# Two PSUM banks for the own-row products, and the one-hots' column numbers in SBUF, in a three-layer graph network

## The reference

```python
# layer 0: graph convolution with self loops, a time embedding, residual, norm
norm = dinv[src] * dinv[dst]                  # dinv = rsqrt(in-degree + 1)
h    = segment_sum(norm[:, None] * (x @ W)[src], dst) + b
x    = layernorm(x + h + (t_emb @ Wt + bt))
# layers 1 and 2: mean of the neighbours and the node's own row
def sage(x, Wl, Wr, b):
    mean = segment_sum(x[src], dst) / max(count, 1)[:, None]
    return mean @ Wl.T + x @ Wr.T + b
x = layernorm(x + sage(relu(sage(x, Wl1, Wr1, b1)), Wl2, Wr2, b2))
```

## Time and profile before

| | before |
|---|---|
| median of three timed runs | 2886.89 us (2882.86 to 2890.46) |
| span of the profiled execution | 3459.0 us |
| busy: TensorE / VectorE / ScalarE / GpSimd | 2757.7 / 1126.8 / 552.0 / 1944.5 us |
| mean granted TensorE clock | 0.902 of full speed |
| bytes moved by DMA | 654.19 MB, 528.61 of them by the gathers |

### The profile page before, as it was taken

How to read it: one execution, slowest core, us unless ns; L and a number is a source line. 1 busy time by engine, 2 the same in 40 slices (tenths; PEclk the granted TensorE clock), 3 DMA queues, 4 the chain that set the end, 5 groups by cost and what they waited for, 6 DMA issues and landing times.

```text
span 3459.0 us, 53711 instructions
## 1 busy us (share of the span) xinstructions
PE 2757.7 (80%) x9822; PEld 1016.0 (29%) x9823; DVE 1126.8 (33%) x2467; ACT 552.0 (16%) x1265; POOL 1944.5 (56%) x2041
## 2 busy tenths in 40 slices
PE   7465676777878888888888787887888888887778
PEld 7212222222222233333332222232333332222222
DVE  8532333333334431112222223231222232333334
ACT  0200111111122211111111111121111111111122
POOL 1266666666555535555666665544555666666553
PEclk9877888888998999999999988999999999988899
DMA  4656566666666645666666666656566666666664
GB/s 167 229 157 177 170 184 190 207 202 208 207 203 184 195 153 174 189 187 200 203 208 203 204 205 199 202 177 196 165 184 179 200 201 190 188 189 188 181 182 139
DMA packets 230235, 654.19 MB, mean 189 GB/s; under 512 B 39294, under 2 KB 40912, under 8 KB 230182
## 3 DMA queue, kind: packets, MB, share of 16 engines
q0 software_dynamic: 161280, 528.61, 52.5%
q1 hardware_dynamic: 46356, 84.02, 6.8%
q10 hardware_dynamic: 22578, 41.30, 3.7%
HBM read 602.43 MB, written 52.15 MB: 189 GB/s over the span
## 4 chain that ended last, share of the span: by engine, by line
PE 38%; issue 23%; another core or an unknown queue 19%; DVEq 7%; DVE 6%; ACTq 4%; ACT 2%; DMA 1%; POOL 0%; SPq 0%; POOLq 0%
PE sum_ps L1330 19%; PE prod_ps L1324 7%; PE root_ps L1341 6%; PE dense_ps L1357 2%; DVEq L907 1%; ACT half_sum L1090 1%; DVEq L363 1%; DVE oh L933 1%; PE root_ps L1213 1%; DMA table<-stage 1%; DVE oh_next L912 1%; DVEq L335 1%; PE selfT_ps L1375 1%; PE sum_ps L1335 1%
## 5 line engine op out<-in xcount | busy, mean ns | idle before, releaser
L558 POOL DMA_INDIRECT raw<-rows,idx_ring x1344 | 1277.9, 951 | 939.8 <-issue 498.3
L1330 PE MATMUL sum_ps<-raw,oh 128*64 128x512 f32 x4032 | 1085.6, 666 | 247.5 <-issue 123.7
L558 POOL DMA_INDIRECT raw<-table,idx_ring x672 | 656.8, 977 | 452.5 <-issue 261.1
L1324 PE MATMUL prod_ps<-W_left,aggT 128*128 128x512 f32 x1176 | 571.7, 631 | 40.7 <-issue 29.2
L1330 PEld LDWEIGHTS sum_ps<-raw,oh 128*64 128x64 f32 x4032 | 294.2, 150 | 901.6 <-issue 895.9
L1341 PE MATMUL root_ps<-W_right,selfT 128*128 128x512 f32 x784 | 383.8, 635 | 83.9 <-issue 32.1
L1330 PE MATMUL sum_ps<-raw,oh_next 128*64 128x512 f32 x1176 | 345.1, 667 | 77.3 <-DVE oh_next L912 68.2
L1090 ACT ACTIVATE half_sum<-sum_ps 64x512 f32<-64x512 f32 x294 | 174.4, 593 | 1396.4 <-remote 691.5
L1324 PEld LDWEIGHTS prod_ps<-W_left,aggT 128*128 128x128 f32 x1176 | 225.6, 202 | 273.2 <-issue 272.6
L884 DVE TENSOR_TENSOR agg<-sum_ps,half_sum 64x512 f32<-64x512 f32 x144 | 98.5, 684 | 465.8 <-ACT half_sum L1090 270.4
L1341 PEld LDWEIGHTS root_ps<-W_right,selfT 128*128 128x128 f32 x784 | 148.9, 200 | 311.8 <-issue 253.9
(11 more groups left out here) (213 smaller groups left out, 1404.8 us busy)
## 6 DMA issues: line engine op xcount, KB each, us to landing
selfbuf<-rows ACTq DMA_DIRECT2D x101, 256.0 KB
raw<-rows,idx_ring POOLq DMA_INDIRECT x1344
selfbuf<-table ACTq DMA_DIRECT2D x50, 256.0 KB
rows<-X SPq DMA_DIRECT2D x49, 256.0 KB
rows<-hbuf SPq DMA_DIRECT2D x49, 256.0 KB
X<-rows SPq DMA_DIRECT2D x49, 256.0 KB
out<-X SPq DMA_DIRECT2D x48, 256.0 KB
table<-stage SPq DMA_DIRECT2D x21, 512.0 KB, 4.6
```

The source lines that it names most:

```text
L558: nc.gpsimd.indirect_dma_start(out=raw[:, n, j, :], out_offset=None, in_=tables[L][:, :], in_offset=bass.IndirectOffsetOnAxis(ap=idx_ring[ ...
L1324: last = mm(product(L, t1), aggT[:, k * P:(k + 1) * P], W[0][:, k, :], start=(k == 0), stop=(k == KD - 1))
L1330: return mm(sum_ps[j * H:(j + 1) * H, bank:bank + D], of[:, j, :], raw[:, n, j, :], start=fresh, stop=False, skip_group_check=True)
```

## The change

`root_ps` gets two banks and `iota_ps` goes; the products take the two banks in turn, by the parity of r + L - 1, and TensorE waits for one addition less. The histogram and the counts keep the first bank, and the transposed edge table moves to the second. The one-hot comparison reads the column numbers from `iota_row`, a bf16 row of 128 numbers that GpSimd has made in SBUF all along; `column_numbers` is dropped.

```diff
-        root_ps = pb("root_ps", [P, D], fp32)
-        iota_ps = pb("iota_ps", [P, D], fp32)
+        root_ps = pb("root_ps", [P, 2 * D], fp32)
         dense_ps = pb("dense_ps", [P, D], fp32)
-        hist_ps = root_ps
+        hist_ps = root_ps[:, 0:D]
-        tmp_ps = [prod_ps, sum_ps[:, D:2 * D], iota_ps, sum_ps[:, 0:D]]
+        tmp_ps = [prod_ps, sum_ps[:, D:2 * D], root_ps[:, D:2 * D], sum_ps[:, 0:D]]
...
+        def own_product(L, r):
+
+            return root_ps[:, bass.ds(((r + (L - 1)) & 1) * D, D)]
...
-            def column_numbers():
-
-                dve.wait_ge(S["tabs_made"], 2)
-                link(v.tensor_copy(iota_ps[:, 0:H], iota_row[:, 0:H]))
...
-                if n == 20:
-                    column_numbers()
...
-                    v.tensor_tensor(tile_of_x(r), root_ps[:, :], b_all[:, :],
+                    v.tensor_tensor(tile_of_x(r), own_product(L, r), b_all[:, :],
                                     ALU.add).then_inc(S["root_added"], 1)
...
-                    v.tensor_tensor(tile_of_x(r), root_ps[:, :], tile_of_x(r),
+                    v.tensor_tensor(tile_of_x(r), own_product(L, r), tile_of_x(r),
                                     ALU.add).then_inc(S["root_added"], 1)
...
-                        iota_ps[:, 0:H].unsqueeze(1).to_broadcast([P, HR * CH, H]),
+                        iota_row[:, 0:H].unsqueeze(1).to_broadcast([P, HR * CH, H]),
                         dst_rel[:, cols].unsqueeze(2).to_broadcast([P, HR * CH, H]),
...
-                        take_counts(i * 2 + half, (root_ps, dense_ps)[half])
+                        take_counts(i * 2 + half, (hist_ps, dense_ps)[half])
...
-                pe.wait_ge(S["root_added"], r + (T * (L - 1) + LAG))
+                pe.wait_ge(S["root_added"], r + (T * (L - 1) + LAG - 1))
                 pe.wait_ge(S["selfT_ready"], r + (T + 1) * (L - 1))
-                by_weights(root_ps[:, :], selfT, 1, S["root_ready"])
+                by_weights(own_product(L, r), selfT, 1, S["root_ready"])
```

More of the change, by code:

```diff
@@ L1402, in count @@
                             skip_runtime_bounds_check_because="counts of batches, bounded by the capped number of edges")[1]
-                        count_window(i * 2 + half, (root_ps, dense_ps)[half], first[0], first[1])
+                        count_window(i * 2 + half, (hist_ps, dense_ps)[half], first[0], first[1])
                     early_blocks(pe, i, count, lambda d: first_layer_dense(d, half))
```

## The result

The changed kernel takes 2918.06 us in the median of 4 runs (2913.5 to 2918.39), the kernel before 2888.68 us beside it. The ratio is 1.0103, 95% interval 1.0091 to 1.0115: slower by 1.0%, 29 us. The prediction said slower by 0.4%, 2898 us, and its range ended at 2913. The direction was right; the size was not: the time lies 5 us above the end of the range.

What follows compares the result with a forecast made beforehand. The prediction took GpSimd's gather queue and TensorE to run close together as the bound. Relaxed wait -1, registers +2, comparison 0 and holds +10 made +11 us on 2886.9, 2898 us, 0.4% slower, range 2878 to 2913.

Steps and rivals of the forecast that it cites:

- the bank picked by a register: Offset computed for each of 98 own-row products on TensorE's queue: +2 us taken, 8 us if nothing covers it.
- the relaxed wait: Own-row product waits for the addition of r - 2, not r - 1: -1 us, since ScalarE's selfT copy is late next.
- the holds: Gathers on GpSimd held by the all-SBUF one-hot comparison: 20 us, of which half, 10 us, reaches the end.
- VectorE's own ones cost nothing: Register instructions for VectorE's addition: no cost, as TensorE runs ahead of VectorE less than before.
- the 257 slot waits: GpSimd's waits for a ring slot, 633 us, before one gather in eight; there most holds would vanish.
- the 34.8 us of the earlier trace: TensorE idle before eight own-row products that began when VectorE's addition came; the second bank's whole prize.
- more idle time ended by selfT: Sign expected at the own-row products: waits for ScalarE's copy of the transposed rows replace waits for VectorE's addition.
- the comparison's own duration: 253 one-hot comparisons on VectorE: 8 to 10 ns more each, 2 to 2.5 us, or nothing; 0 taken.
- The 65 ns less: Skill-page estimate for each VectorE comparison with an SBUF source, 16 us over 253; left out of the sum.
- Covered: Rival: TensorE stays late with landed gathers before it, or the comparison is exempt; 2888 us, no change; chance 0.22.
- the second bank pays: Rival: waits in early layers 1 and 2 vanish, 29 us scaled; 2859 us, or 2869 with holds; chance 0.12.
- GpSimd is the bound throughout: Rival: every hold counts and the registers too, 20 + 8 - 1, 2914 us; chance 0.16.

Runs made afterwards that it cites:

- iota_alone: Against the kernel before: only the column numbers moved to SBUF, with one bank and the old wait; 2898.95 us, ratio 1.0047.
- pick_early: Against the changed kernel: TensorE computes the bank's offset ahead of the two waits; 2914.43 us, 1.0102 of the kernel before.
- bank_by_branch: Against the changed kernel: TensorE picks the bank by a branch between two fixed copies of the products; 2922.06 us, 1.0121 of the kernel before.
- register_pe_only: iota_alone with an always-zero offset computed by register on TensorE only, VectorE's address fixed; 2913.54 us, 1.0098 of the kernel before.
- register_dve_only: iota_alone with an always-zero offset computed by register on VectorE only, TensorE's address fixed; 2905.39 us, 1.0062 of the kernel before.
- one_bank_by_register: Against the changed kernel: old wait, and the register's offset always picks the first bank; 2913.63 us, 1.0101 of the kernel before.
- old_wait: Against the changed kernel: two banks, but the product waits for the addition of r - 1 again; 2912.12 us, 1.0096 of the kernel before.
- twice_sbuf: Kernel before plus a second, unread comparison per half block with column numbers from SBUF; 2903.69 us, 1.0064.
- twice_psum: Kernel before plus a second, unread comparison per half block with column numbers from PSUM; 2890.73 us, 1.0017.
- the second profile: The kernel before, unedited, run and profiled once more; 2890.97 us in one run, profiled span 2889.2 us.
- split_4: Against the changed kernel: each one-hot comparison in four instructions of 128 columns; 2909.29 us, 1.0085 of the kernel before.
- counts_from_psum: Against the kernel before: layer 0's two count one-hots read their column numbers from PSUM instead of SBUF; 2871.78 us, 0.9951.

## Why the prediction was wrong

**What failed: the bank picked by a register,** "I take +2 us", with 8 us "if nothing covers them". The runs put it at 14 to 16 us above iota_alone, 15 us with the register on TensorE alone. With nothing for the relaxed wait and 13 us for the holds that makes the 29 us. "VectorE's own ones cost nothing" is not refuted: 4 us, with intervals that overlap. The term went by the instructions' durations, two a round at 42 ns each, and took three quarters of that as covered by running matmuls. After the change TensorE's sequencer shows, at the products' line (count, ns min/median/max):

```profile
L1337 PEldq ALU_OP  x147: 32/36/36, 1055.6 to 2600.0; - x147
L1337 PEldq FUSED_REGOPS  x98: 46/51/62, 1055.7 to 2600.2; - x98
```

By durations that is 147 x 36 + 98 x 51 ns = 10.3 us, already above the bound. In the trace they stand about 0.1 us apart, 2.5 in a round. Many are covered, as the prediction thought: in 57 of the 98 rounds (61 before) the first matmul begins without a stop of TensorE. Where TensorE does stop, its stop grows by more than their durations: in the 16 rounds in which the first matmul waits for ScalarE's copy, 68 ns pass on average from the copy's end to the matmul before the change and 347 ns after (in the median 53 and 288). These numbers of single rounds are laid out from the traces by time.

Which of the added instructions costs is not shown. In pick_early that gap is 204 ns on average and in bank_by_branch 245, but the stops of the other rounds are longer there (30.4 and 33.9 us in all, against 27.4 in the changed kernel), and the time does not fall. What the runs show is the price of choosing the bank at run time on TensorE's queue, wherever in the round that is done.

Idle time ahead of the products and their own busy time, from the groups by line, add up to about what the runs lost. Two more of these lines, of register_pe_only:

```profile
L1337 PE MATMUL root_ps<-W_right,selfT 128*128 128x512 f32 x784 | 367.5, 612 | 46.0 <-issue 30.9 <-ACT selfT L1092 14.0 <-ACT selfT L1065 1.0
```

and of bank_by_branch:

```profile
L1337 PE MATMUL root_ps<-W_right,selfT 128*128 128x512 f32 x784 | 373.1, 620 | 47.9 <-issue 35.8 <-ACT selfT L1092 10.3 <-ACT selfT L1065 1.6
```

| kernel | idle before + busy, us | above iota_alone | ratio above iota_alone, of 2887 us |
|---|---|---|---|
| iota_alone | 32.5 + 365.6 | 0 | 0 |
| register_dve_only | 37.5 + 369.2 | 8.6 | 4 |
| register_pe_only | 46.0 + 367.5 | 15.4 | 15 |
| pick_early | 43.8 + 370.3 | 16.0 | 16 |
| one_bank_by_register | 47.0 + 369.2 | 18.1 | 16 |
| old_wait | 45.3 + 370.8 | 18.0 | 14 |
| the change | 43.1 + 372.7 | 17.7 | 16 |
| bank_by_branch | 47.9 + 373.1 | 22.9 | 21 |

One column is of one profiled execution, the other of the runs, so a few us between them mean nothing. Both put iota_alone first, then register_dve_only, then five kernels that neither column tells apart, and bank_by_branch last.

The products' matmuls also run longer in the mean (609 to 619 ns), while their minimum and median, 592 ns, are the same before and after. The trace shows what makes the mean: 22 of the 784 records of the changed kernel take over 1.0 us, most of them 1.06; there are 7 in iota_alone. They lie in stretches in which the granted TensorE clock is 0.5, 1.2 of 2.4 GHz, as from 1113.4 to 1116.8 us; in the trace of iota_alone the same stretch has 1.0. They belong to five rounds, before whose first matmul TensorE had stood still for 1.9 to 2.5 us (one such round in iota_alone); other rounds with such a stop have none. register_pe_only has only 9 such records, so this part differs from kernel to kernel while the time hardly does.

How the 16 us divide to the last few stays open. In the trace of after the first lot of gathers is 6.7 us longer than in iota_alone (873.1 and 866.4 us from the first to the last start), where no own-row product runs; in register_pe_only it is 867.4. Over the kernels with the same count one-hots that lot goes from 863.9 to 873.1 us, so one profiled execution says no more than that.

**Right: the holds, and half of them.** 20 us forecast, 10 of them in the end; iota_alone measures 13, twice_sbuf over twice_psum 13 as well. The trace of iota_alone has 21.9 us of holds inside the comparison. They were laid out by layer: in layers 1 and 2 the comparison holds 17.4 us, and the two lots of rows take 10.7 us longer from the first to the last start (1808.2 before, 1818.9 in iota_alone); the rest is taken out of GpSimd's waits for a slot. In layer 0 each gather begins 0.3 us after the end of the one before, so GpSimd never waits for a slot there, yet the lot is no longer (865.9 and 866.4 us): the comparison's 4.5 us came with some 4 us less of the other holders' (the normalisation of layer 0 and the count one-hots). That offset is of this one execution: in twice_sbuf the lot is 6.9 us longer than in twice_psum (870.8 and 863.9), with 6.6 us of holds inside the added comparison in layer 0. So "half" was right as a number, and its reason (some holds where a slot wait follows) is seen in layers 1 and 2 only; the 257 slot waits that it was argued from were of the long execution, and in the second profile no gather of layer 0 begins later than the usual 0.3 us after the one before. That the number came out so near is in part luck.

The Trainium skill, "SBUF — State Buffer", section "Who interferes with whom", infers that descriptor generation isn't held by a tensor_tensor. The trace disagrees, now for the comparison as for L844: 0.69 us of VectorE, and a gather of 1.24 us in place of 0.95 (L929 and L561 above). By the page iota_alone and twice_sbuf would have been as fast as their controls; they are 13 us slower.

**Right in substance: the relaxed wait.** -1 us was put down, old_wait measures nothing. But its rows were of one long execution: the 34.8 us of the earlier trace rows are not in the second profile, so there was no such wait to win in the runs. What the prediction looked for there, more idle time ended by selfT, hardly came: 9.6 + 1.6 us before, 12.9 + 0.9 after, while "issue" grew from 20.4 to 29.1.

**Right: the comparison's own duration,** 682 to 685 ns for 253, +0.7 us of VectorE. The 65 ns less that were estimated from the Trainium skill ("VectorE: DVE Perf Modes", the section on the TRN2 errata) are not seen.

**The rivals.** "Covered" and "the second bank pays" fell with iota_alone and old_wait. "GpSimd is the bound throughout" gave 2914 us, the nearest number, by the wrong way: in after, GpSimd's gathers of layers 1 and 2 still wait for slots for 92 us beyond the usual 0.3 us between two, only in layer 0 do they never wait, and the register's price falls on TensorE. That 2914 lies nearest is luck. No rival had the register alone cost more than the holds.

## What to carry to other kernels

For an engine that is near the bound, don't price an address that is computed in a loop by its instructions' durations alone: here they came to 10.3 us and the runs lost 14 to 16, 0.15 us a round. Moving the computation ahead of a wait or making it a branch did not help. Leaving one bank did; unrolling by two with fixed banks would avoid the address too, but no run here tried it. Where GpSimd issues gathers, look at which VectorE instructions have both operands in SBUF: put one operand in PSUM, and begin with the stretch in which GpSimd never waits. Before resting a sum on a wait, take a profile whose span stands near the timed median.

## What the runs showed that was not expected

A held gather ends 0.81 to 0.83 us after VectorE's instruction (77 of them in iota_alone), whatever was left of that when it started; where the next instruction with both operands in SBUF follows at once, it can be held through that one as well (split_4). And two holders that were there all along cost as much as the new one: taking the count one-hots' operands out of SBUF (counts_from_psum) shortened the first lot of gathers by 16.8 us.
